# Expert stage of a fused two-layer program: the four transposes of the next expert's tokens move ahead of the transposes of the inner values in TensorE's order

## What is computed

```python
scores = softmax(xf @ router_w.T)                 # 2048 tokens x 64 experts
topk_w, topk_idx = top_k(scores, 8)               # 8 experts for each token
topk_w = topk_w / (topk_w.sum(-1) + 1e-20)
...                                               # at most 128 tokens per expert
gate = einsum('ech,ehf->ecf', xb, w_gate)         # xb: 64 x 128 x 512, f = 192
up = einsum('ech,ehf->ecf', xb, w_up)
hmid = silu(gate) * up
yb = einsum('ecf,efh->ech', hmid, w_down)         # back to width 512
...                                               # weighted, added to the token's row
x = x + tanh(g_ffn[1]) * out
```

## Time and profile before

| | |
|---|---|
| median of 3 runs | 2991.49 us (2989.27 to 3000.47) |
| the profiled execution, its own time | 2993.2 us |
| its span from first to last instruction | 2991.4 us |
| PE, DVE, ACT, POOL busy, share of the span | 88%, 58%, 43%, 27% |
| mean granted TensorE clock | 0.946 of full speed |
| expert stage: first gather issued | 2576.65 us from the start |
| expert stage: last result scaled | from 2956.64 us |

### The profile page before, as it was taken

The page is one execution under the profiler, slowest core; times in us unless marked ns, Lnnn a source line. Parts: engine busy times, 40 slices in busy tenths (PEclk is TensorE's granted clock), DMA queues, the critical chain, the costliest instruction groups (busy, mean ns, idle before and its releaser), DMA issues. The chain is left out here.

```text
span 2991.4 us, 48203 instructions
## 1 busy us (share of the span) xinstructions
PE 2631.3 (88%) x17077; PEld 2104.6 (70%) x17099; DVE 1724.2 (58%) x3837; ACT 1272.2 (43%) x3385; POOL 807.8 (27%) x827
## 2 busy tenths in 40 slices
PE   6998987589998699999699999999999984489895
PEld 4665654579997588887588888888888864255552
DVE  7767766853342666666566666666666656422221
ACT  3767665222221444444455555555555541022121
POOL 3231311000000355555222222222222220244443
PEclk8999998889999799999799999999999996699997
DMA  3011000510000555555721421331241108899986
GB/s 127 19 43 47 23 19 19 162 41 29 15 29 29 187 189 189 187 191 183 218 52 51 136 55 42 109 85 43 78 121 43 43 27 271 257 294 297 292 193 111
DMA packets 227119, 340.06 MB, mean 114 GB/s; under 512 B 24641, under 2 KB 111041, under 8 KB 226369
## 3 DMA queue, kind: packets, MB, share of 16 engines
q1 hardware_dynamic: 211968, 297.11, 32.1%
q0 software_dynamic: 14912, 39.85, 6.5%
HBM read 230.56 MB, written 110.53 MB: 114 GB/s over the span
## 5 line engine op out<-in xcount | busy, mean ns | idle before, releaser
L1744 POOL TENSOR_SCALAR a_prob<-a_prob,a_rinv 128x640 f32<-128x640 f32 (+3 forms) x256 | 252.5, 986 | 768.0 <-DVE a_rinv L1899 768.0
L1889 DVE TENSOR_REDUCE a_mx<-a_s_ps 128x1 f32<-128x640 f32 (+3 forms) x256 | 262.2, 1024 | 274.1 <-PE a_s_ps L1813 267.9
L1765 ACT ACTIVATE a_probT<-a_t_ps 128x512 fp32r<-128x512 f32 (+3 forms) x512 | 237.1, 515 | 367.7 <-PE a_t_ps L1821 367.7
L1905 DVE TENSOR_TENSOR a_probT<-a_t_ps,a_probT 128x512 fp32r<-128x512 f32 (+3 forms) x512 | 276.5, 582 | 47.5 <-ACT a_probT L1765 47.3
L1756 ACT ACTIVATE a_prob<-a_s_ps,a_nb,a_rs 128x640 f32<-128x640 f32 (+3 forms) x256 | 267.8, 1046 | 0.0
L137 PE MATMUL a_o_ps<-a_probT,a_v 128*128 128x256 f32 x832 | 245.3, 295 | 0.0
L138 PE MATMUL a_o_ps<-a_probT,a_v 128*128 128x256 f32 x832 | 235.0, 283 | 0.0
L139 PE MATMUL a_o_ps<-a_probT,a_v 128*128 128x256 f32 x832 | 235.0, 282 | 0.0
L1821 PE MATMUL a_t_ps<-a_ident,a_prob 128*128 128x128 f32 x1664 | 225.4, 274 | 8.0 <-DVE a_probT L1905 5.0
L137 PE MATMUL f_bank<-f_xT,f_gu 128*128 128x256 f32 x704 | 202.6, 288 | 22.0 <-DVE f_gu L1152 22.0
L1821 PEld LDWEIGHTS a_t_ps<-a_ident,a_prob 128*128 128x128 f32 x1664 | 194.1, 141 | 30.7 <-issue 5.1
(11 more groups left out here) (299 smaller groups left out, 6769.6 us busy)
## 6 DMA issues: line engine op xcount, KB each, us to landing
m_ring<-in_w_gate SPq DMA_DIRECT2D x64, 384.0 KB, 5.8
m_ring<-in_w_up SPq DMA_DIRECT2D x64, 384.0 KB, 7.3
m_ring<-in_w_down SPq DMA_DIRECT2D x64, 384.0 KB, 9.6
l_q_hi<-p_turned SPq DMA_DIRECT2D x64, 256.0 KB, 2.7
l_q_lo<-p_turned SPq DMA_DIRECT2D x64, 256.0 KB, 2.8
a_qT<-l_q_hi SPq DMA_DIRECT2D x64, 256.0 KB, 3.6
a_qT<-l_q_lo SPq DMA_DIRECT2D x64, 256.0 KB, 4.2
l_v_hi<-p_vs SPq DMA_DIRECT2D x32, 256.0 KB, 2.6
```

The source lines that it names most:

```text
L1744: pool.tensor_scalar(prob[:, k % 4, 0:w], prob[:, k % 4, 0:w], rinv[:, k % 4:k % 4 + 1], 1.0, ALU.mult, ALU.mult).then_inc(s["weighted"], 1)
L1765: act.activation(probT[0][:, pair % 2, i * 4:i * 4 + n, k % 2], t_ps[i][:, 0:n * P].rearrange("p (m n) -> p m n", n=P), ACT.Copy).then_inc ...
L1889: step(dve.tensor_reduce(mx[:, k % 4:k % 4 + 1], s_ps[:, k % 2, 0:w], AX.X, ALU.max))
L1905: dve.tensor_tensor(probT[1][:, pair % 2, i * 4:i * 4 + n, k % 2], t_ps[i][:, 0:n * P].rearrange("p (m n) -> p m n", n=P), probT[0][:, pai ...
```

## The change

In PE's program `turn_x(e + 1)` is called directly behind `gate_up(e)`, ahead of `turn_h(e - 1)`; before, it stood between `turn_h(e - 1)` and `down(e - 1)`. Nothing is added or removed, and the other engines' programs are the same.

```diff
--- before.py
+++ after.py
@@ -2354,10 +2354,9 @@
                 for e in range(E + 1):
                     if e < E:
                         gate_up(e)
+                    turn_x(e + 1)
                     if e:
                         turn_h(e - 1)
-                    turn_x(e + 1)
-                    if e:
                         down(e - 1)
 
             @block.vector
```

## The result

The changed kernel takes 3009.82 us (median of 6 runs, 3002.03 to 3014.54), the kernel before, in 6 runs, 2990.38 (2982.29 to 3000.47). The ratio is 1.0062, with a 95% interval of 1.0037 to 1.0086: slower by 0.6%, 19 us. The forecast of 3000 had the sign and the tail right, the range of 2991 to 3013 held the time, and the likeliest case was half the true size. The profiled execution took 3013.02 us with a span of 3010.9. One execution of a later run (e7) had a granted clock of 0.729 over the whole program and took 3459.47 us; it is left out of that run's figures.

What follows compares the result with a forecast made beforehand. Full DMA engines, about 5.9 us an expert, were taken as the loaded part's bound, PE as the tail's. Front +0.5, loaded part +1 and tail +7.0 made +8.5 on 2993.2, 3001.7, less 1.7: 3000 us, range 2991 to 3013.

Steps and rivals of the forecast that it cites:

- the sign: Whole kernel: the change was forecast to make it slower, by 0.28%.
- the tail: Expert stage from the gather at 2881.93 us on, PE the bound: about 14 iterations at +0.50 us, +7.0 us.
- the likeliest case: Whole kernel: the forecast itself, sum +8.5 us, 3000 us, own range 2995 to 3005, chance 0.70.
- The front: Expert stage, iterations 1 to 3, before transfers pile up: the first load comes 0.50 us later, +0.5 us.
- The landing time of 7.1 us: Loaded part: gathers would land about 7 us after issue instead of 7.5.
- the loaded part: Expert stage while weights are loaded, 45 experts of 5.93 us: pace kept by full DMA engines, +1 us.
- the gather's loop: Loaded part: from one gather's issue to the next over two experts, 11.76 us, forecast to grow by 0.77.
- +1, cover: the full DMA engines: Loaded part: full engines hide the longer loop; +1 us for backlog no longer carried when the loads end.
- Its upper bound, 17: Loaded part: cost in us if the cover is not there, 45 x 0.77 / 2.
- the first rival: Loaded part: the gather's delay, not engine throughput, is the limit; loops grow 0.77 us, +26 in all, 3017 us; chance 0.15.
- Something halfway: Whole kernel: a result between the forecast and the first rival, around 3009 us; chance 0.06.
- The doubt that I set aside: Routing moved 382 GB/s at the same DMA share of 1.05; taken as another transfer mix, not this mix's ceiling.

Runs made afterwards that it cites:

- e7: Kernel before, with SP issuing the load for expert e + 17 only once the gather for expert e + 4 has landed; 3016.06 us, ratio 1.0097.
- e5: Kernel before with six token buffers in place of four, the result buffers staying four; 2961.48 us, ratio 0.9904.
- e9: Kernel before with five token buffers in place of four, the result buffers staying four; 2958.18 us, ratio 0.9887.
- e3: Kernel before with only the wait for the gather of expert e + 1 moved ahead of turn_h, transposes left in place; 3000.23 us, ratio 1.0023.
- e4: Kernel before with four extra transposes of a constant ahead of turn_h in iterations 1 to 62, turn_x left in place; 2993.50 us, ratio 1.0003.
- e10: Kernel before with six token buffers and turn_h moved ahead of the last quarter of gate_up; 2942.26 us, ratio 0.9832.

## Why the prediction was off in size

**What held.** The transposes cost nothing where they stood and 0.475 us where they went (I took 0.50); the tail and the end cost 5.4 and 0.9 us, 6.3 in all against 7.0. The front cost 0.9 against 0.5. The wait of 0.47 us for the copy stands ahead of each down product. ACT's copies and DVE's steps, called hidden, are waited for nowhere else. The landing time of 7.1 us came as forecast.

**What failed** is the step that read the loaded part: "the DMA engines are full, each expert costs them about 5.9 us, and the gather's delay only stretches until the loop fits". The first clause is true (share 1.05, and still 1.06 in e5), and so, nearly, is the second: 298 GB/s in e5 make it 5.8 us. The step from there to the pace, and the third clause, are not. The pace was the gather's loop divided by two, which came out within 2% of the engines' price, and I took the one for the other. More buffers alone brought 5.254 (e5, e9), with the engines as full as before. So the term "+1, cover: the full DMA engines" measured +9.9. Its upper bound, 17, was the loop's growth paid in full.

**Luck.** The range held because the loop's growth was paid only in part. Paid in full it gives the first rival's 3017 us, outside the range. Something halfway, "around 3009", is what was measured, and it had a chance of 0.06 and no mechanism.

**The first rival** was the right mechanism. Its price, 45 times half of 0.77, came out at little more than half: the rest of the loop grew by 0.96 us in the pair shown, even more than the 0.77, but the gather landed 0.4 us sooner. The profile before also holds the one iteration of 8.9 us, some 2.7 more than its neighbours with a wait, and the changed kernel's holds none, so the +9.9 is if anything too small. e3 shows that the wait alone, with the work left in place, costs; e4 that the work alone, with the wait left in place, does not. The two measured +0.23% and +0.03%, and together +0.6%, so they do not simply add. In the changed kernel all four transposes and the bare copy stand behind the late gather (0.86 us more), whereas in e3 only 0.27 do, and in e4 the extra work is done before the gather is due. Why the gather gave back 0.4 us at the slower pace was not isolated; that less is in flight then is only argued.

**The doubt that I set aside** was the row with 382 GB/s, and I had no row that showed anyone waiting for weights. A full resource whose users can lag behind a deep ring is not a bound until the ring's lead is gone. The trace of before said so: no wait for weights appears in it, every wait for a transfer on PE is for the gather. The figure in the Trainium skill, DMA: Bandwidth & Descriptors, Specifications, about 358 GB/s, led to the right rival, but not by the right sum. By it an expert costs the engines an estimated 4.85 us, less than PE's period; at the 298 GB/s of e5 it is 5.8, more than that. The trace does not agree with the figure on either side: with full engines this stage moved 284 to 307 GB/s, and routing, without indirect transfers, 382.

## What to carry to other kernels

Busy is not bound: before a full DMA queue is called the limit, ask who waits for what it carries. Here the weights could lag by 56 us unnoticed while a gather of 7.4 us, issued too late by one buffer, paced the stage; one more buffer gave some 30 us. How long such a lag goes unpaid is set by the ring: with 8 experts in place of 17, and more bytes, PE had to wait. And a short filler between a producer and the copy it waits for is worth its place: moved ahead, it costs its whole length (0.475 us here), since the wait that it covered stands bare again, and behind a late transfer's wait it lengthens the loop as well.

## What was unexpected in the hardware

- A long wait of PE costs twice. Before, one iteration took 8.9 us: PE stood idle for 2.00 us on a gather, and then the granted clock was 0.57 of full speed in the window behind it, near the lower level of 1.2 GHz, with a down product of 3.50 us in place of 1.88:

```profile
2842.00:2846.00 4.00, 4.00 (x9) 1.80 (x9) 0.98 (x3) 0.82 (x2) 0.00 (x0) 0.57 1.04 299
```

  In e7, after an idle time of 3.35 us, it was 0.50 and 3.62 us. The changed kernel's profile has no such iteration (clock 1.00 through the loaded part), e3's has three.
- The DMA share reads 1.04 to 1.06 at 284, 298, 307 (e10) and 382 GB/s alike; once it is at its top it says nothing of the rate that is left.
- More work for PE at an even pace (e4) made the loaded part 6 us faster than less work at an uneven one.
